# Four graph networks in one kernel: VectorE's next-tile work in front of the preceding tile's candidate

## The chip, the cores and the metric

The kernel runs on one core of one Trainium2 chip. The metric is the device time of one execution in microseconds; a lower time is better. Engines are called PE (TensorE, matmuls), DVE (VectorE), ACT (ScalarE), POOL (GpSimd) and SP (SyncE, which only issues transfers). Each has its own queue of instructions and works through it in order; they meet through semaphores.

## The reference

A graph has 12,500 nodes with 64 features and 212,500 edges (source, destination, type 0 to 3, weight). Four networks follow each other, each with a residual and a layer norm:

```python
x = layernorm(x + L0(x))   # 4 steps: a = segment_sum((x W_k + b_k)[type, src], dst); x = GRU(a, x)
x = layernorm(x + L1(x))   # 2 GIN convolutions: mlp(x + segment_sum(x[src], dst))
x = layernorm(x + L2(x))   # GCN: segment_sum(norm * (x W)[src], dst), relu, batch norm over all nodes
x = layernorm(x + L3(x))   # SAGE mean with edge weights

def _gru_cell(a, feat, w_ih, w_hh, b_ih, b_hh):
    gi = a @ w_ih.T + b_ih
    gh = feat @ w_hh.T + b_hh
    r, z = sigmoid(i_r + h_r), sigmoid(i_z + h_z)
    n = jnp.tanh(i_n + r * h_n)
    return (1.0 - z) * n + z * feat
```

All of it is a sum of source rows over the edges of each destination, and then a small dense part for each destination node.

## The kernel before

After a setup that sorts the edges into slots, the kernel makes nine passes (`p`), each over the 98 tiles (`NT`) of 128 destination nodes. Passes 0 to 3 are the four GRU steps, 4 to 6 the GIN layers, 7 is the GCN convolution, 8 the SAGE layer. Loops over tiles are unrolled.

One tile's sum has three sources. First, eight tiles ahead, PE picks source rows with one-hot matmuls into `ps_pair` (`oct_`, L1177, two for each step), ACT copies them to `raw_f` (`copy_pair`, L1479) and stores them to HBM in `bounce_f` (`move_out`, L1490). Six such steps make a group. SP loads a tile's 120 rows back in destination order into `thirds` (`load_msgs`, L791); ahead of a group's first tile it waits on SP's queue until all stores of the group have landed. Second, DVE splits these fp32 values into three bf16 parts: `split_rest` (L2050) makes the second part and waits for the load (`rows_back`), `split_low` (L2055) makes the third and reports `parts_made`. PE's `grid` (L1213) multiplies them with one-hots of the destination, which pass 0 makes on DVE (`make_grid`, L2013) and stores, which passes 1 to 3 load, and which later passes make anew. Third, edges that found no slot are gathered by POOL (L999) and summed by PE with left-over one-hots (`left_over_batch`, L1235), made on DVE by `make_left` (L2030, in pass 7 L2036 and L2040). The last of its four batches reports `tile_summed`.

Then comes the dense part, one tile behind. DVE adds the sums up (`take_sums`, L2081 in passes 0 to 3, L2094 in pass 7), PE turns them (`turn_sums`, L1252) and multiplies by the weights (`first_product`), ACT makes the gates with a tanh (L1530, `gate_done`), DVE makes the candidate's argument (`candidate`, L2162 and L2165), ACT its tanh (L1543, `cand_done`), and DVE mixes the new state (`finish`, L2177 and on). In pass 3 ACT loads a table ahead of the gate's tanh and another ahead of the square root of the layer norm. The new rows are split into three bf16 parts as well, by `late_parts`: its third entry, `low_of` (L2149), is in pass 3 the one that follows behind the candidate.

In pass 7 `candidate` is another computation: it waits for `gate_summed`, makes `o` (L2169), adds a bias row to `xs` (L2171), and ACT's relu of `o` (L1537) gives the row of `hs`. PE's `second_product` sums that row into the batch mean (L1294); in pass 7 it stands in PE's queue between the third and the fourth `left_over_batch`. In passes 4, 5, 6 and 8 `candidate` does nothing.

DVE's order is written out by hand in `one_tile`: with `at` as the tile whose sums PE makes, it takes the sums of `prev` (one back), does late parts of `older` (two back), and makes what PE needs for the next tile (`more`). In ACT's `one_tile` the order is: pair copy 0, turned copy, own rows, gate tanh or relu, candidate tanh, pair copy 1, store of the step.

Of the kernel before, what the change touches and what calls it, by code (L numbers as in the profile page):

```python
# [82 lines left out]
def build(nc, x, src, dst, edge_type, edge_weight, g_W, g_b, g_w_ih, g_w_hh, g_b_ih, g_b_hh,  # L83
# [53 lines left out]
    def tops(x):  # L137

        return x.rearrange("p x g f -> p (x g f)").bitcast(bf16).rearrange(
            "p (x g f o) -> p x g f o", x=3, f=H, o=2)[:, :, :, :, 1]  # L140
# [455 lines left out]
    def turns(at):  # L596
        return at.i * 6 + NT * len([q for q in range(at.p) if q != P_GIN2A]) + at.jj + 1
# [1081 lines left out]
    def _(dve):  # L1679
# [304 lines left out]
        def tile(t, at):  # L1984
            return t[:, ds(at.d(), 1), :].rearrange("p o f -> p (o f)")
# [13 lines left out]
        def make_grid(at, more):  # L1999
            if at.p in KEPT:  # L2000
                return
            if at.p == 0 and not (isinstance(at.i, int) and at.jj + more < 3):
                dve.wait_ge(doh_moved[at.slot3(more)], at.uses3(more) * 16)
                dve.sem_inc(dve_ran, 1)
            to = halves((doh_kept[at.slot3(more)] if at.p == 0 else doh_one[at.half(more)])[0:ROWS], GB)
            keep = dict(saturate=False) if at.p == 0 else {}
            lanes = dl_all[0:ROWS, ds(at.d(more), 1), :].rearrange("p o n -> p (o n)")
            if at.p == 0 and not isinstance(at.i, int):
                fixed = left_ws[0][0:ROWS].rearrange("p a g -> p (a g)")
                v.tensor_copy(fixed, lanes)  # L2010
                dve.drain()
                lanes = fixed
            last = v.tensor_tensor(to, numbers(ROWS, GB), spread(lanes, ROWS, GB), ALU.is_equal, **keep)  # L2013
            if at.p == P_SAGE:
                n, ws = (at.jj + more) % 3, edge_ws[at.half(more)][0:ROWS]
                dve.wait_ge(grec_landed[n], at.i * 32 + ((at.jj + more) // 3 + 1) * 16)
                for a in range(3):
                    v.tensor_copy(ws[:, a, :].rearrange("p (g o) -> p g o", o=2), twice(grec[n][0:ROWS, a, :], ROWS, GB))
                dve.drain()
                for a in range(3):  # L2020
                    last = v.tensor_tensor(halves(doh_three[at.half(more)][0:ROWS, a * GB * P:(a + 1) * GB * P], GB), to,  # L2021
                                           spread(ws[:, a, :], ROWS, GB), ALU.mult)
            last.then_inc(doh_made, 1)

        def make_left(at, more):
            rec, ws, hots = lrec[at.slot6(more)], left_ws[at.half(more)], loh_at[at.half(more)]
            dve.wait_ge(lrec_landed[at.slot6(more)], at.uses6(more + 6) * 16)
            if at.p < P_GIN1:
                for b in range(LB):
                    last = v.tensor_scalar(hots[:, b * K * P:(b + 1) * K * P], iota512[:, :],  # L2030
                                           rec[:, b, 2:3], None, ALU.is_equal)
                last.then_inc(loh_made, 1)
                return
            weights = range(3) if at.p == P_SAGE else ()
            for a, f in [(3, DL)] + [(a, W0 + a) for a in weights]:
                v.tensor_copy(ws[:, a, :].rearrange("p (g o) -> p g o", o=2), twice(rec[:, 0:LB, f], P, LB))  # L2036
            dve.drain()  # L2037
            plain = 3 if at.p == P_SAGE else 0
            to = [halves(hots[:, a * LB * P:(a + 1) * LB * P], LB) for a in range(4)]
            last = v.tensor_tensor(to[plain], numbers(P, LB), spread(ws[:, 3, :], P, LB), ALU.is_equal)  # L2040
            if at.p == P_SAGE:
                dve.drain()
                for a in weights:
                    last = v.tensor_tensor(to[a], to[3], spread(ws[:, a, :], P, LB), ALU.mult)
            last.then_inc(loh_made, 1)

        def split_rest(at, more):
            x = thirds[at.two(more)][0:ROWS]
            dve.wait_ge(rows_back[at.two(more)], at.backs(more) * 16)
            v.tensor_tensor(x[:, 1, :, :], x[:, 0, :, :], tops(x)[:, 0, :, :], ALU.subtract)  # L2050

        def split_low(at, more):
            x = thirds[at.two(more)][0:ROWS]
            dve.drain()
            v.tensor_tensor(x[:, 2, :, :], x[:, 1, :, :], tops(x)[:, 1, :, :], ALU.subtract).then_inc(parts_made, 1)  # L2055

        def take_state(at):
            if P_GIN1 <= at.p < P_SAGE:
                v.tensor_reduce(out=own_x[at.half()][:, :],
                                in_=tile(rows_now, at).rearrange("p (a f) -> p f a", a=3), axis=AX.X, op=ALU.add)  # L2060
            if at.p in (P_GIN2B, P_SAGE):
                v.tensor_copy(state[at.half()][:, 0:H], tile(hs if at.p == P_GIN2B else xs, at))
# [96 lines left out]
        def candidate(at):  # L2159
            if at.p < P_GIN1:  # L2160
                dve.wait_ge(gate_done, at.tiles(1))
                v.scalar_tensor_tensor(out=cand[:, :], in0=gate[:, 0:H], scalar=1.0, in1=ps_gate[:, 3 * H:4 * H],  # L2162
                                       op0=ALU.add, op1=ALU.mult)
                dve.drain()
                v.scalar_tensor_tensor(out=cand[:, :], in0=cand[:, :], scalar=0.5, in1=ps_gate[:, 2 * H:3 * H],  # L2165
                                       op0=ALU.mult, op1=ALU.add).then_inc(cand_made, 1)
            elif at.p == P_GCN:
                dve.wait_ge(gate_summed, turns(at))
                v.scalar_tensor_tensor(out=o[:, :], in0=ps_gate[:, 0:H], scalar=rsqrt_n[:, ds(at.d(), 1)],  # L2169
                                       in1=conv_b[:, :], op0=ALU.mult, op1=ALU.add).then_inc(o_biased, 1)  # L2170
                v.tensor_tensor(tile(xs, at), tile(xs, at), bn_beta[:, :], ALU.add)  # L2171
# [116 lines left out]
        def one_tile(at, careful=False):  # L2288
            p, known = at.p, isinstance(at.i, int)
            prev = None if known and at.jj == 0 else At(p, at.jj - 1, at.i)  # L2290
            older = None if known and at.jj < 2 else At(p, at.jj - 2, at.i)
            more = not (known and at.jj == NT - 1)
            if prev is not None:
                take_sums(prev, careful)
            if older is not None:
                late_parts[p][0](older)
            if more:
                make_grid(at, 1)
            if more and at.joined():
                split_rest(at, 1)  # L2300
            if older is not None:
                late_parts[p][1](older)
            take_state(at)
            if prev is not None:
                candidate(prev)
            if more:
                make_left(at, 1)
            if more and at.joined():
                split_low(at, 1)
            if older is not None:  # L2310
                late_parts[p][2](older)
            if prev is not None:
                finish(prev)
# [66 lines left out]
        for p in range(NPASS):  # L2380
# [18 lines left out]
            if p in range(1, P_SAGE):  # L2399
                for a in range(7):  # L2400
                    dve.wait_ge(rows_loaded[a], 16 * p)
            one_tile(At(p, 0))
            full = dve.value_load(any_full[0:1, 0:1], min_val=0, max_val=1)
            with dve.If(full < 1):
                long_loop(dve, p, 1, one_tile)
                take_sums(At(p, NT - 1))
            with dve.If(0 < full):
                by_six(dve, p, lambda at: one_tile(at, True), check_six)
                take_sums(At(p, NT - 1), True)
# [35 lines left out]
```

## Time and profile before

| | us |
|---|---|
| median of 3 runs | 9118.53 (9115.04 to 9126.54) |
| the profiled execution | 9112.42, span 9110.5 |
| busy, of the span | PE 72%, DVE 80%, ACT 41%, POOL 55% |
| chain that ended last | DVE 46%, DVEq 14%, PE 14%, DMA 11%, issue 8%, ACT 6% |

The span is the time from the first to the last instruction on record. Busy shares are means over passes with different limits; the chain that ended last says which engine the end was waiting for, followed back from the last instruction (DVEq is DVE's sequencer). What a change to one pass is worth is read from that pass's own rows.

### The profile page before, as it was taken

Reading aid. Unit: us, or ns where it says so; the run is one execution under the profiler, and the core shown is the slowest. Engines: PE = TensorE matmul, PEld = TensorE weight load, DVE = VectorE, ACT = ScalarE, POOL = GpSimd, SP = SyncE. Lnnn points to the kernel's source line nnn. Section 1 sums busy time; section 2 is a strip of 40 time slices with the busy share of each in tenths; the row PEclk is TensorE's granted clock in tenths of the full one; section 3 lists DMA queues with packets and bytes.
Section 4 is the critical chain, followed back from the end, with each engine's and each line's share of the span. In section 5 each row is a group of like instructions: output and inputs, shape, how many; then the busy total and the mean of one; then the engine's idle time right before and its main releaser. Section 6 shows DMA issues by size and latency. Waiting matters only on the chain.

```text
span 9110.5 us, 225080 instructions
## 1 busy us (share of the span) xinstructions
PE 6559.6 (72%) x82141; PEld 5404.3 (59%) x82142; DVE 7331.1 (80%) x16597; ACT 3714.5 (41%) x9508; POOL 5049.9 (55%) x4223
## 2 busy tenths in 40 slices
PE   3766676577777777777777778766667767748888
PEld 2333333477666666666666666655556656627777
DVE  8999999699977776776766678867779978859998
ACT  1444444444444444444666643321123322234443
POOL 2545455455545554554444457768877757744443
PEclk7999999899999999999888888978789989969999
DMA  3211121477778888888666778888788888848887
GB/s 90 74 60 53 54 64 53 141 195 195 196 214 221 219 225 223 220 220 227 177 175 177 182 217 236 241 229 218 217 228 209 212 220 231 235 123 221 216 219 182
DMA packets 1210397, 1665.55 MB, mean 183 GB/s; under 512 B 413276, under 2 KB 856575, under 8 KB 1206386
## 3 DMA queue, kind: packets, MB, share of 16 engines
q1 hardware_dynamic: 969618, 994.91, 41.9%
q10 hardware_dynamic: 126656, 482.46, 15.3%
q0 software_dynamic: 113056, 174.29, 9.8%
q8 instruction: 629, 10.31, 0.5%
q14 instruction: 438, 3.59, 0.1%
HBM read 1062.93 MB, written 588.17 MB: 181 GB/s over the span
## 4 chain that ended last, share of the span: by engine, by line
DVE 46%; DVEq 14%; PE 14%; DMA 11%; issue 8%; ACT 6%; POOL 2%; SPq 0%; ACTq 0%; POOLq 0%
DVE work L2055 8%; DMA work<-bounce_f 5%; DVE agg_sb L2081 4%; DVE work L2030 4%; DVE work L2013 4%; DVEq L2037 3%; DMA bounce_f<-work 3%; PE ps_agg L1213 3%; DVE hs L2021 2%; DVE work L2050 2%; PE ps_gate L1273 2%; DVE work L1822 2%; DVEq L1839 2%; ACT turned L1508 2%; PE ps_pair L1177 2%
## 5 line engine op out<-in xcount | busy, mean ns | idle before, releaser
L999 POOL DMA_INDIRECT work<-node_rows,work x3528 | 4203.4, 1191 | 3030.5 <-DMA work<-left_recs 1613.7
L1213 PE MATMUL ps_agg<-work 120*128 120x192 bf16 x12544 | 1348.5, 260 | 731.0 <-DVE work L2055 728.4
L1177 PE MATMUL ps_pair<-rows_now,work 128*128 128x64 bf16 x39168 | 1557.6, 201 | 141.2 <-DMA work<-src_onehots 69.7
L1213 PEld LDWEIGHTS ps_agg<-work 120*128 120x128 fp8e4 (+1 forms) x12544 | 1138.9, 101 | 809.8 <-issue 789.5
L1177 PEld LDWEIGHTS ps_pair<-rows_now,work 128*128 128x128 fp8e4 x39168 | 1477.4, 103 | 211.9 <-issue 160.3
L1479 ACT ACTIVATE work<-ps_pair 120x512 f32<-120x512 f32 x1632 | 954.2, 585 | 862.2 <-PE ps_pair L1177 750.0
L2050 DVE TENSOR_TENSOR work<-work 120x1024 f32<-120x1024 f32 x784 | 959.3, 1224 | 334.6 <-DMA work<-bounce_f 324.2
L2055 DVE TENSOR_TENSOR work<-work 120x1024 f32<-120x1024 f32 x784 | 961.8, 1227 | 75.8 <-issue 4.5
L1235 PE MATMUL ps_agg<-work 128*128 128x192 bf16 (+1 forms) x7840 | 901.9, 260 | 166.1 <-DMA work<-node_rows,work 165.9
L2013 DVE TENSOR_TENSOR work<-iota_bf,dl_all 120x2048 bf16<-120x2048 bf16 (+1 forms) x588 | 824.2, 1402 | 27.9 <-SPq L746 15.3
L1235 PEld LDWEIGHTS ps_agg<-work 128*128 128x128 bf16 x7840 | 672.5, 104 | 198.7 <-issue 157.2
L2081 DVE TENSOR_TENSOR agg_sb<-agg_sb,ps_agg 128x256 f32<-128x256 f32 x1176 | 493.5, 420 | 65.0 <-PE ps_agg L1235 3.7
L953 POOL TENSOR_SCALAR work<-work 128x36 f32<-128x36 f32 x49 | 90.6, 1850 | 784.8 <-PE ps_pair L1105 567.0
L2162 DVE SCALAR_TENSOR_TENSOR cand<-gate,ps_gate 128x64 f32<-128x64 f32 x392 | 86.4, 220 | 514.8 <-ACT gate L1530 511.8
L2030 DVE TENSOR_SCALAR work<-iota,work 128x512 bf16<-128x512 int16 x1568 | 493.0, 377 | 0.8 <-issue 0.7
L1483 ACT ACTIVATE work<-ps_pair 120x384 bf16<-120x384 f32 x816 | 368.4, 485 | 272.9 <-PE ps_pair L1190 260.7
L1508 ACT ACTIVATE turned<-ps_turn 128x384 f32<-128x384 f32 (+2 forms) x784 | 316.2, 403 | 373.0 <-PE ps_turn L1264 241.0
L1273 PE MATMUL ps_gate<-state_w,turned 69*128 69x256 f32 x784 | 304.1, 473 | 226.3 <-ACT turned L1508 226.3
L1221 PE MATMUL ps_agg<-work,hs 120*128 120x192 bf16 x4704 | 454.5, 246 | 5.3 <-DMA work<-bounce 2.9
L1447 ACT ACTIVATE work<-hs,ones_f 128x480 fp8e4<-128x480 bf16 x392 | 409.4, 1137 | 8.1 <-ACT hs L1439 4.2
L1221 PEld LDWEIGHTS ps_agg<-work,hs 120*128 120x128 bf16 x4704 | 393.3, 97 | 8.8 <-issue 3.2
L955 POOL TENSOR_SCALAR work<-hs 128x36 f32<-128x36 f32 x196 | 387.3, 2033 | 0.0
(345 smaller groups left out, 11715.8 us busy)
## 6 DMA issues: line engine op xcount, KB each, us to landing
bounce_f<-work ACTq DMA_DIRECT2D x816, 480.0 KB
work<-bounce_f SPq DMA_DIRECT2D x784, 480.0 KB
work<-src_onehots SPq DMA_DIRECT2D x918, 256.0 KB
bounce<-work ACTq DMA_DIRECT2D x102, 727.5 KB
work<-bounce SPq DMA_DIRECT2D x98, 727.5 KB
work<-dst_onehots SPq DMA_DIRECT2D x294, 240.0 KB
work<-node_rows,work POOLq DMA_INDIRECT x3528
hs<-grid_vals SPq DMA_DIRECT2D x49, 960.0 KB, 5.0
```

Source lines behind the costliest of these rows:

```text
L999: pool.indirect_dma_start(out=ring[:, at.slot6() * LB + b, 0:3 * H], out_offset=None, in_=table_of(at.p), in_offset=bass.IndirectOffsetOnA ...
L1177: last = mm(to[:, a * H:(a + 1) * H], oh[s.buf()][:, EIGHT * m + a, :], rows_now[:, s.chunk() * CHUNK + EIGHT * m + a, x * H:(x + 1) * H], ...
L1213: last = mm(acc[:, to:to + 3 * H], hot, tops(thirds[at.two()])[0:ROWS, :, b, :], start=b == 0 or p < P_GIN1 and b == GB // 2, stop=False)
L1221: mm(acc[:, 0:3 * H], doh_three[at.half()][0:ROWS, (a * GB + b) * P:(a * GB + b + 1) * P], msgs[at.jj % 3][0:ROWS, k, s, 0:3 * H], start=a ...
L1235: last = mm(acc[:, k * AGG:k * AGG + n], hot, ring[:, u * LB + b, 0:n], start=False, stop=end and (p >= P_GIN1 or k % 2 == 1))
L1479: a_(raw_f[s.raw()][0:ROWS, 2 * m:2 * m + 2, :, :], ps_oct[s.bank(m)][0:ROWS, :].rearrange("p (i b f) -> p i b f", i=2, b=SB), ACT.Copy).t ...
L1508: a_(to, frm, ACT.Copy).then_inc(turned_copied, 1)
L2013: last = v.tensor_tensor(to, numbers(ROWS, GB), spread(lanes, ROWS, GB), ALU.is_equal, **keep)
L2030: last = v.tensor_scalar(hots[:, b * K * P:(b + 1) * K * P], iota512[:, :], rec[:, b, 2:3], None, ALU.is_equal)
L2050: v.tensor_tensor(x[:, 1, :, :], x[:, 0, :, :], tops(x)[:, 0, :, :], ALU.subtract)
L2055: v.tensor_tensor(x[:, 2, :, :], x[:, 1, :, :], tops(x)[:, 1, :, :], ALU.subtract).then_inc(parts_made, 1)
L2081: last = v.tensor_tensor(to, to, typed[:, :, x * H:(x + 1) * H], ALU.add)
```

## The change

In DVE's `one_tile`, the block that makes the next tile's left-over one-hots (`make_left`) and its second split (`split_low`) is now ahead of the candidate of the preceding tile; before, it was behind it.

```diff
@@ -2301,12 +2301,12 @@
             if older is not None:
                 late_parts[p][1](older)
             take_state(at)
-            if prev is not None:
-                candidate(prev)
             if more:
                 make_left(at, 1)
             if more and at.joined():
                 split_low(at, 1)
+            if prev is not None:
+                candidate(prev)
             if older is not None:
                 late_parts[p][2](older)
             if prev is not None:
```

No instruction is added, removed or resized, and no semaphore changes its count. The other engines' queues are as they were.

## Rows read from the trace of the kernel before

**Rows 1.** Waits of DVE, whole span: line, releaser, us, times, longest.
```profile
DVE cand L2162 <- ACT gate L1530: 511.8, 310, 3.5
```

**Rows 2.** Windows, passes 0, 1, 3, 7: length, busy (xtiles), PEclk, DMA share, GB/s.
```profile
1760.00:2600.00 840.00, 20.62 (x93) 0.92 0.72 197
2720.00:3400.00 680.00, 18.60 (x84) 1.00 0.80 220
...
4340.00:5200.00 860.00, 19.07 (x86) 0.85 0.69 176
...
7450.00:8000.00 550.00, 31.14 (x87) 0.92 0.87 233
```

**Rows 3.** Timeline of DVE, pass 1: start, us, line; idle before in brackets.
```profile
2906.10 1.45 DVE L2081 TENSOR_TENSOR agg_sb<-agg_sb,ps_agg 128x256 f32<-128x256 f32 x3
...
2907.60 1.22 DVE L2050 TENSOR_TENSOR work<-work 120x1024 f32<-120x1024 f32 x1
...
2910.43 0.22 DVE L2162 SCALAR_TENSOR_TENSOR cand<-gate,ps_gate 128x64 f32<-128x64 f32 x1 [1.47 <-ACT gate L1530]
2910.73 0.22 DVE L2165 SCALAR_TENSOR_TENSOR cand<-cand,ps_gate 128x64 f32<-128x64 f32 x1
2910.87 1.39 DVE L2030 TENSOR_SCALAR work<-iota,work 128x512 bf16<-128x512 int16 x4
2912.35 1.23 DVE L2055 TENSOR_TENSOR work<-work 120x1024 f32<-120x1024 f32 x1
2913.49 0.22 DVE L2177 TENSOR_TENSOR delta<-state,cand_t 128x64 f32<-128x64 f32 x1
...
2914.23 0.91 DVE L2081 TENSOR_TENSOR agg_sb<-agg_sb,ps_agg 128x256 f32<-128x256 f32 x2
```

**Rows 4.** Waits of DVE in pass 0 alone, 1744 to 2640 us.
```profile
DVE cand L2162 <- ACT gate L1530: 17.3, 21, 2.2
```

**Rows 5.** Timeline of the other engines, pass 1, the same tile and its neighbour.
```profile
2907.61 0.33 PE L1252 MATMUL ps_turn<-eye,agg_sb 128*128 128x128 f32 x1 [0.48 <-DVE agg_sb L2081]
...
2910.98 0.26 ACT L1543 ACTIVATE cand_t<-cand 128x64 f32<-128x64 f32 x1 [0.58 <-DVE cand L2165]
...
2911.83 0.32 ACTq L1490 DMA_DIRECT2D bounce_f<-work  x1
...
2913.72 1.52 PE L1213 MATMUL ps_agg<-work 120*128 120x192 bf16 x16 [0.91 <-DVE work L2055]
```

**Rows 6.** Timeline of ACT and of DVE at a group's start, pass 7.
```profile
7672.87 0.32 ACTq L1490 DMA_DIRECT2D bounce_f<-work  x1
...
7684.15 1.23 DVE L2050 TENSOR_TENSOR work<-work 120x1024 f32<-120x1024 f32 x1 [2.63 <-DMA work<-bounce_f]
```

**Rows 7.** One window in and behind that wait, pass 7; columns PE, PEld, DVE, ACT, POOL.
```profile
7683.00:7690.00 7.00, 4.04 (x42) 3.66 (x40) 5.52 (x11) 1.34 (x3) 3.59 (x4) 0.61 1.02 285
```

**Rows 8.** Timeline of DVE, one tile of pass 3.
```profile
4799.25 1.41 DVE L2081 TENSOR_TENSOR agg_sb<-agg_sb,ps_agg 128x256 f32<-128x256 f32 x3
...
4804.62 0.22 DVE L2162 SCALAR_TENSOR_TENSOR cand<-gate,ps_gate 128x64 f32<-128x64 f32 x1 [2.03 <-ACT gate L1530]
...
4809.15 1.41 DVE L2081 TENSOR_TENSOR agg_sb<-agg_sb,ps_agg 128x256 f32<-128x256 f32 x3
```

**Rows 9.** Timeline of DVE, PE and ACT, one tile of pass 7.
```profile
7603.11 0.28 DVE L2169 SCALAR_TENSOR_TENSOR o<-ps_gate,rsqrt_n,conv_b 128x64 f32<-128x64 f32 x1
...
7603.43 0.42 DVE L2036 CAST work<-work 128x8 bf16<-128x8 f32 x1
...
7604.00 0.25 PE L1235 MATMUL ps_agg<-work 128*128 128x192 bf16 x1
...
7604.26 0.36 ACTq L1490 DMA_DIRECT2D bounce_f<-work  x1
...
7604.45 1.22 DVE L2055 TENSOR_TENSOR work<-work 120x1024 f32<-120x1024 f32 x1
...
7605.76 0.36 DVE L2094 TENSOR_REDUCE agg_sb<-ps_agg 128x64 f32<-128x192 f32 x1
```

## The prediction

> **What bounds the kernel now.** I read four views in this order. The waits of VectorE (DVE) come first: its one large wait inside the passes is for ScalarE's gate tanh, just in front of the candidate, 511.8 us over 310 tiles [rows 1]. Four windows of steady stretches give each pass its period as length by count: 840/93 = 9.03 us a tile in pass 0, 680/84 = 8.10 in pass 1 (pass 2 is its twin), 860/86 = 10.00 in pass 3, 550/87 = 6.32 in pass 7 [rows 2]. The other passes have no candidate, so the edit leaves their order alone. The timeline of one tile of pass 1 then shows a closed loop: DVE takes the sums at 2906.10, is out of work 1.47 us before the gate at 2910.43, and starts the next sums at 2914.23 without waiting for them, 8.13 us later [rows 3]. So in passes 1 to 3 the way sums, turn (PE), copy (ACT), product (PE), gate (ACT), back to DVE sets the period, with DVE's remaining work behind it. In pass 0 DVE has its one-hot grid to make in between, and waits for the gate only 17.3 us in all [rows 4].
>
> **Part 1: one-hots and second split move ahead of the candidate, passes 1 and 2.** Nothing is added or removed; on DVE only the order of two blocks changes, and no DMA is issued by either. Times from the start of the sums, t0. The moved block starts where DVE falls idle, at 2910.43 - 1.47 = 2908.96, t0 + 2.8 or so. From L2030 to the step behind L2055 it takes 2913.49 - 2910.87 = 2.62 us, more than the 1.47 us wait, so the candidate starts at about t0 + 5.4 and never waits for its gate (which was there at t0 + 4.33) [rows 3]. Gain: 1.47. The new cost: `finish` now stands directly behind the candidate and needs ScalarE's tanh of it. L2165 to the tanh is 0.25 us, the tanh 0.26 [rows 3, 5], and some 0.03 back: 0.54 us from L2165 to L2177, where L2165 to L2030 took 0.14. Cost 0.40. An instruction that doesn't wait also starts 0.08 before its predecessor ends (L2030 at 2910.87, L2165 until 2910.95), which the waiting one loses. By DVE alone the tile takes 8.13 - 1.47 - 0.08 + 0.40 = 6.98 us. PE fits: of its 8.13 us it waits 0.91 for the split and 0.48 for the sums [rows 5], so it has 6.7 us of work at full clock, 0.25 under the new period.
>
> What is late next is not on DVE. ScalarE's queue holds, behind the candidate's tanh, the second pair copy and the store of a step's rows to `bounce_f` (L1490), 0.85 us after the tanh starts [rows 5]. Every sixth tile the SP queue may load the next group only when that store has landed, and DVE's first split two tiles on needs the load. Today the store goes out at 2911.83, 2.40 us before the next sums, and the split comes 8.13 + 1.50 us after those: 12.0 us are available [rows 3, 5]. After the change the tanh starts at t0 + 5.95, the store at 6.80, only 0.17 before the next sums: 0.17 + 6.98 + 1.50 = 8.65 us are available. What the round trip takes shows in pass 7 under like traffic: store at 7672.87, the split that waited for its data at 7684.15, 11.3 us [rows 6]. So 2.7 us are lost every sixth tile, 0.44 a tile: 7.42. Such a stall leaves PE idle, and in pass 7 the granted clock after a wait of this kind is 0.61 of full speed over 7 us, mostly the 1.2 GHz level [rows 7]; pass 1, with PE's short waits of today, is at the 2.4 GHz level throughout (1.00 [rows 2]). With 0.25 us of slack PE then holds DVE up by 1 to 2 us: I add 0.2 a tile. Estimate 7.62 us against 8.10, gain 0.48 x 97 tiles x 2 passes = 93 us. Bounds: 6.98 (no stall, 109 a pass) and 8.1 (nothing).
>
> The Trainium skill would have it otherwise. In "DMA: Bandwidth & Descriptors", section "Anatomy of one DMA", a transfer costs about 2.0 us and its bytes at 436 GB/s; for the 120 x 1024 fp32 of a step an estimate by that page is 3.1 us each way, 6.3 for both, and no stall at all. The trace disagrees: 11.3 us [rows 6], with the DMA engines at 0.87 of the time [rows 2]. The measured one is used; the page's result is rival B.
>
> **Part 2: pass 3.** The wait for the gate is 2.03 us in a tile of 4809.15 - 4799.25 = 9.90 [rows 8], because its gate also sits behind a table load. The moved block, 2.5 us as before, takes its place, and here `low_of` stands between candidate and `finish` and hides part of the tanh: cost 0.26 instead of 0.40, by one slot of 0.14. 9.90 - 2.03 - 0.08 + 0.26 = 8.05, if the gate, there at t0 + 5.37, comes before the moved block ends at t0 + 5.6. The mean period of 10.00 holds tiles with a slow PE clock (0.85 [rows 2]); with the gate off the path most of that goes. DMA need rises from 0.69 to 0.69 x 10.00/8.15 = 0.85, just bearable. I take 8.15: 1.85 x 97 = 180 us gained. Bounds: 190 (8.05 throughout) and 130 (a period of 8.65, PE's slow tiles staying).
>
> **Part 3: pass 0** pays the 0.40 and has little wait to give back: 0.40 x 98 = 39, less 17.3 [rows 4] = 21 us lost (bounds 5 and 40).
>
> **Part 4: pass 7.** Here the candidate is `o`, its consumer ScalarE's relu, and behind that PE's mean product, which PE issues ahead of the last left-over product that ends the tile's sum. Now: `o` at 7603.11, last product 7604.00 to 7604.25, next sums 7605.76; DVE is never waiting and the sum is 1.5 us early [rows 9]. After: L2055 starts 0.32 earlier (what L2169 and L2171 took), at 7604.13, `o` 1.14 later at 7605.27, which is 2.16 later than now; the tile's sum ends 2.16 later too, 7606.41, next sums 7606.47 instead of 7605.76. That is 0.71 us a tile, a wait of DVE for PE that did not exist. The store moves with the relu from 1.50 us ahead of the sums to 0.05 ahead while the period grows 0.71, so the group's stall grows by 0.74, 0.12 a tile. 0.83 x 98 = 81; DMA is less loaded at the longer period, so I take 75 us lost (bounds 40 and 95).
>
> **Sum.** +21 - 93 - 180 + 75 = -177 us. The profiled execution took 9112.4 us with a span of 9110.5; the median of the runs is 9118.5. The change scales neither the 2 us around the span nor the setup, so it is taken off the median: 9118.5 - 177 = 8941, say 8940.
>
> **Rivals.** A, the above, 50%. B, the group's round trip shrinks or hides and passes 1 and 2 reach 6.98: 21 - 218 - 180 + 55 = -322, 8800 us, 15%. For it: today's regular loads are never waited for in pass 1. Against it: the 11.3 us [rows 6]. C, DMA and PE's clock eat the gain of passes 1 and 2 altogether and pass 3 gives 140: 21 + 0 - 140 + 80 = -39, 9080 us, 22%. For it: 0.80 x 8.10/6.98 = 0.93 of DMA time would be needed, and no steady stretch shows over 0.87 [rows 2]. D, slower: PE's clock. PE needs 6.7 us a tile at 2.4 GHz [rows 5] and at most twice that, 13.4, at 1.2 GHz. If stalls hold it low for 30% of passes 1 to 3 the tile takes 8.7: 2 x 0.6 x 97 = +116, pass 3 -126, passes 0 and 7 +96 as above, sum +86, 9205 us. It decides from about a quarter of the time on; the clocks of 0.85 and 0.92 in passes 3 and 7 mean 30 and 16% [rows 2], pass 1 shows none. 8%. The Trainium skill speaks for D: "TensorE: Matmul & The Clock Gate", "HAM oscillation", warns that a loop that waits for a transfer each round starts each round cold. The trace agrees for one round [rows 7], but here it is one tile in six. E, the order changes and the wait only changes its name (the tanh copy waits as long as the gate did): 9118, 5%; against it ScalarE is idle ahead of that tanh [rows 5].
>
> A and B are faster, C mostly (0.2% is 18 us, about what a measurement of this kernel can tell from no change): faster 0.86, same 0.06, slower 0.08. Range 8820 to 9085: A with its bounds, C, and the part of B where a stall of a microsecond is left; B's far end and D stay out, under 2 in 10.
>
> **What would show it.** DVE's wait in front of L2162 gone in passes 0 to 3 and one of about 0.3 us at L2177 from ScalarE's tanh (part 1). L2050 waiting for `bounce_f` every sixth tile of passes 1 and 2, 2 to 4 us (if absent, B). Periods 9.2, 7.6, 8.15 and 7.1 us. In pass 7 a wait of DVE's L2094 for PE's L1235. Granted clock under 1.00 in passes 1 and 2, nearer 1.00 in pass 3. It would be wrong if the round trip is far from 11 us, or if in pass 3 ScalarE's table loads come back onto the path.

## The result: 8867 us, and the profile after

| | before | after |
|---|---|---|
| median of 4 runs each, us | 9117.24 (9115.04 to 9126.54) | 8866.99 (8864.22 to 8878.84) |
| the profiled execution, us | 9112.42, span 9110.5 | 8868.43, span 8866.5 |

The ratio is 0.9726, with a 95% interval from 0.9709 to 0.9743: 250 us faster, where 177 were forecast. The spans differ by 244 us. To see where they went, each pass is measured from the start of its first sums (L2081, in passes 4 to 8 L2094) to the start of its last, 97 tiles later. The same table holds the experiments below (us, one profiled execution each):

| kernel | pass 0 | 1 | 2 | 3 | 4 | 5 | 6 | 7 |
|---|---|---|---|---|---|---|---|---|
| before | 879.2 | 781.8 | 781.7 | 973.2 | 651.1 | 645.4 | 703.9 | 613.2 |
| after | 901.6 | 717.8 | 708.8 | 796.8 | 645.8 | 647.3 | 701.9 | 662.2 |
| e1_gcn_old | 901.4 | 721.7 | 722.4 | 794.9 | 637.3 | 644.1 | 704.5 | 606.7 |
| e2_store_first | 901.1 | 700.6 | 700.0 | 796.1 | 648.9 | 638.8 | 702.6 | 670.8 |
| e3_half | 870.0 | 691.1 | 698.8 | 871.3 | 664.5 | 639.2 | 705.6 | 617.3 |
| e4_light_dma | 902.6 | 681.8 | 688.7 | 797.0 | 644.3 | 643.7 | 702.2 | 658.1 |
| e5_tanh_twice | 914.1 | 700.8 | 702.2 | 811.9 | 650.0 | 644.4 | 704.7 | 650.5 |
| e6_before_light | 882.3 | 773.0 | 770.6 | 973.6 | 638.2 | 638.0 | 705.2 | 603.0 |
| f1_split_behind | 869.7 | 689.4 | 683.0 | 793.7 | 658.6 | 652.3 | 701.9 | 612.7 |
| f2_store_too | 866.4 | 689.6 | 693.1 | 795.5 | 657.0 | 641.9 | 705.4 | 606.6 |
| g1_before_store | 884.2 | 783.7 | 780.0 | 975.0 | 663.9 | 647.5 | 708.9 | 617.0 |
| g2_before_swap | 882.9 | 786.6 | 784.7 | 973.4 | 651.4 | 648.4 | 710.5 | 619.4 |

Passes 4 to 6, which no kernel here changes, show the scatter of such a number: up to 27 us in pass 4, 14 in pass 5, 9 in pass 6. Passes 1 and 2 scatter as well: e1 has the order of after in them (717.8 and 721.7, 708.8 and 722.4 us), f1 that of e3 (691.1 and 689.4, 698.8 and 683.0). So a difference of 15 us in one pass shows nothing by itself. The kernels also ran at different times and on different chips: the before that ran beside them took 9117 us beside after, 9125 beside e1 to e4, 9110 beside e5, e6, f1 and f2, and 9139 beside g1 and g2. Ratios are taken against that one, and are the better comparison between experiments. Between before and after, pass 0 lost 22 us, passes 1 and 2 won 64 and 73, pass 3 won 176, pass 7 lost 49. That is 242 of the 244.

The waits of VectorE (line, releaser, us in all, times, longest) answer [rows 1]:

```profile
DVE work L2050 <- DMA work<-bounce_f: 407.2, 230, 31.5
DVE agg_sb L2094 <- PE ps_agg L1235: 113.2, 114, 4.2
DVE delta L2177 <- ACT cand_t L1543: 112.4, 389, 0.3
...
DVE cand L2162 <- ACT gate L1530: 23.7, 11, 3.7
```

The wait for the gate fell from 511.8 us to 23.7. Three others grew: for ScalarE's tanh, at 0.29 us each in all four GRU passes; for PE's sums, where the prediction put it (28.2 us in before); and for the loads from `bounce_f`, which before took 324.2 us over 134 waits.

The windows of steady stretches answer [rows 2] (length; busy and count of L2165, in pass 7 of L2094; PE clock; DMA share; GB/s). First passes 0, 1, 2 and 3, then pass 7:

```profile
1800.00:2600.00 800.00, 18.84 (x85) 0.88 0.73 190
2720.00:3400.00 680.00, 20.39 (x92) 0.97 0.91 243
3480.00:4140.00 660.00, 19.95 (x90) 0.97 0.93 247
4220.00:4980.00 760.00, 20.57 (x93) 0.92 0.83 220
```
```profile
7150.00:7750.00 600.00, 31.44 (x88) 0.84 0.84 216
```

Periods are 717.8/97 = 7.40 us in pass 1, 708.8/97 = 7.31 in pass 2, 796.8/97 = 8.21 in pass 3, 662.2/97 = 6.83 in pass 7 and 901.6/97 = 9.29 in pass 0. The DMA engines now work at 0.91 to 0.93 of the time in passes 1 and 2, above all that before had shown [rows 2].

One undisturbed tile of pass 2 stands against [rows 3] (timeline of DVE: start, us, line, idle before and releaser):

```profile
3580.30 1.40 DVE L2081 TENSOR_TENSOR agg_sb<-agg_sb,ps_agg 128x256 f32<-128x256 f32 x3
...
3581.75 1.22 DVE L2050 TENSOR_TENSOR work<-work 120x1024 f32<-120x1024 f32 x1
...
3583.02 1.14 DVE L2030 TENSOR_SCALAR work<-iota,work 128x512 bf16<-128x512 int16 x4
3584.25 1.23 DVE L2055 TENSOR_TENSOR work<-work 120x1024 f32<-120x1024 f32 x1
3585.39 0.21 DVE L2162 SCALAR_TENSOR_TENSOR cand<-gate,ps_gate 128x64 f32<-128x64 f32 x1
3585.68 0.22 DVE L2165 SCALAR_TENSOR_TENSOR cand<-cand,ps_gate 128x64 f32<-128x64 f32 x1
3586.22 0.22 DVE L2177 TENSOR_TENSOR delta<-state,cand_t 128x64 f32<-128x64 f32 x1 [0.32 <-ACT cand_t L1543]
...
3586.97 1.41 DVE L2081 TENSOR_TENSOR agg_sb<-agg_sb,ps_agg 128x256 f32<-128x256 f32 x3
```

The block fills the place of the wait, L2162 runs at once, and L2177 starts 0.54 us after L2165: as forecast. The tile takes 6.67 us, not the 6.98 of the sum. Most of that is seen in the row of L2030: its four instructions take 1.14 us here from the first's start to the last's end, 1.39 in [rows 3].

A group's start in pass 2 (ScalarE's store, SP's load, and the split that waits for it) answers [rows 6]:

```profile
3480.20 0.32 ACTq L1490 DMA_DIRECT2D bounce_f<-work  x1
```
```profile
3485.55 0.34 SPq L791 DMA_DIRECT2D work<-bounce_f  x1
```
```profile
3490.78 1.23 DVE L2050 TENSOR_TENSOR work<-work 120x1024 f32<-120x1024 f32 x1 [2.17 <-DMA work<-bounce_f]
```

This round trip takes 10.58 us. "Round trip" is here the time from the issue of a group's last store to the start of the first split that uses its rows; it holds two transfers, the wait on SP's queue and DVE's wait. Over 15 groups of a pass (without the first and the last) its mean is 10.2 in pass 1 and 10.1 in pass 2, and the idle time in front of the split is 1.45 and 1.36 us, where before had 0.00. In pass 7 the round trip went from 11.4 us before to 9.6 after, and the idle time from 2.39 to 1.15.

A tile of pass 3 of after (DVE) answers [rows 8], and one of pass 7 (several engines) [rows 9]:

```profile
4502.29 1.41 DVE L2081 TENSOR_TENSOR agg_sb<-agg_sb,ps_agg 128x256 f32<-128x256 f32 x3
4503.62 0.15 DVE L2122 RECIPROCAL rstd<-std 128x1 f32<-128x1 f32 x1
...
4507.94 0.21 DVE L2162 SCALAR_TENSOR_TENSOR cand<-gate,ps_gate 128x64 f32<-128x64 f32 x1
4508.23 0.22 DVE L2165 SCALAR_TENSOR_TENSOR cand<-cand,ps_gate 128x64 f32<-128x64 f32 x1
4508.37 0.22 DVE L2149 TENSOR_TENSOR stage<-left_over,stage 128x64 bf16<-128x64 f32 x1
4508.77 0.23 DVE L2177 TENSOR_TENSOR delta<-state,cand_t 128x64 f32<-128x64 f32 x1 [0.19 <-ACT cand_t L1543]
```
```profile
7302.56 1.23 DVE L2055 TENSOR_TENSOR work<-work 120x1024 f32<-120x1024 f32 x1
7303.70 0.28 DVE L2169 SCALAR_TENSOR_TENSOR o<-ps_gate,rsqrt_n,conv_b 128x64 f32<-128x64 f32 x1
...
7304.01 0.26 ACT L1537 ACTIVATE hs<-o 128x64 f32<-128x64 f32 x1 [3.39 <-DVE o L2169]
...
7304.32 0.43 PE L1294 MATMUL ps_agg<-hs,mean_f 128*128 128x64 f32 x2 [2.16 <-ACT hs L1537]
...
7304.59 0.25 PE L1235 MATMUL ps_agg<-work 128*128 128x192 bf16 x1
...
7304.86 0.32 ACTq L1490 DMA_DIRECT2D bounce_f<-work  x1
7304.88 0.36 DVE L2094 TENSOR_REDUCE agg_sb<-ps_agg 128x64 f32<-128x192 f32 x1 [0.77 <-PE ps_agg L1235]
```

In pass 3 the candidate no longer waits, and what is left of the tanh is 0.19 us, since L2149 lies in between. In pass 7 the chain is the one that was forecast, link by link: `o` behind L2055, relu, mean product, last left-over product, sums, each waiting for the one above; the store goes out at the sums and not 1.50 us ahead of them.

### The profile page after: what moved, and what is told of

It reads as the page before. It is cut to its first block, busy times and chain, and to the rows that moved or that the text cites. A ratio compares the mean times of both kernels' runs of the same rounds, so it can differ in the third digit from the quotient of the medians.

```text
span 8866.5 us, 225080 instructions
## 1 busy us (share of the span) xinstructions
PE 6555.1 (74%) x82141; PEld 5433.4 (61%) x82142; DVE 7299.7 (82%) x16597; ACT 3712.4 (42%) x9508; POOL 5050.2 (57%) x4223
## 4 chain that ended last, share of the span: by engine, by line
DVE 45%; DMA 16%; DVEq 14%; PE 11%; issue 8%; ACT 3%; POOL 2%; SPq 1%; ACTq 0%; POOLq 0%
DMA work<-bounce_f 9%; DVE work L2055 7%; DMA bounce_f<-work 4%; DVE work L2013 4%; DVE work L2050 4%; DVE work L2030 3%; DVE agg_sb L2081 3%; DVEq L2037 3%; PE ps_agg L1213 3%; DVE hs L2021 3%; PE ps_pair L1177 2%; POOL work L999 2%; DVE work L1822 2%; DVEq L1839 2%; DVE work L1814 2%
## 5 line engine op out<-in xcount | busy, mean ns | idle before, releaser
L999 POOL DMA_INDIRECT work<-node_rows,work x3528 | 4211.5, 1194 | 2765.1 <-DMA work<-left_recs 1310.3
L1177 PE MATMUL ps_pair<-rows_now,work 128*128 128x64 bf16 x39168 | 1582.9, 202 | 143.4 <-DMA work<-src_onehots 71.0
L1213 PE MATMUL ps_agg<-work 120*128 120x192 bf16 x12544 | 1369.6, 262 | 371.4 <-DVE work L2055 370.7
L1177 PEld LDWEIGHTS ps_pair<-rows_now,work 128*128 128x128 fp8e4 x39168 | 1502.5, 104 | 218.1 <-issue 166.8
L2050 DVE TENSOR_TENSOR work<-work 120x1024 f32<-120x1024 f32 x784 | 957.5, 1221 | 418.1 <-DMA work<-bounce_f 407.2
L2055 DVE TENSOR_TENSOR work<-work 120x1024 f32<-120x1024 f32 x784 | 961.6, 1226 | 75.9 <-issue 4.5
L2081 DVE TENSOR_TENSOR agg_sb<-agg_sb,ps_agg 128x256 f32<-128x256 f32 x1176 | 493.1, 419 | 79.7 <-PE ps_agg L1235 13.2
L1273 PE MATMUL ps_gate<-state_w,turned 69*128 69x256 f32 x784 | 299.2, 466 | 230.5 <-ACT turned L1508 230.5
L2030 DVE TENSOR_SCALAR work<-iota,work 128x512 bf16<-128x512 int16 x1568 | 460.3, 356 | 0.1
L1543 ACT ACTIVATE cand_t<-cand 128x64 f32<-128x64 f32 x392 | 100.5, 256 | 737.5 <-DVE cand L2165 733.4
```

Of the source, the lines that this page charges most:

```text
L999: pool.indirect_dma_start(out=ring[:, at.slot6() * LB + b, 0:3 * H], out_offset=None, in_=table_of(at.p), in_offset=bass.IndirectOffsetOnA ...
L1177: last = mm(to[:, a * H:(a + 1) * H], oh[s.buf()][:, EIGHT * m + a, :], rows_now[:, s.chunk() * CHUNK + EIGHT * m + a, x * H:(x + 1) * H], ...
L1213: last = mm(acc[:, to:to + 3 * H], hot, tops(thirds[at.two()])[0:ROWS, :, b, :], start=b == 0 or p < P_GIN1 and b == GB // 2, stop=False)
L2081: last = v.tensor_tensor(to, to, typed[:, :, x * H:(x + 1) * H], ALU.add)
```

## Experiments

**e1_gcn_old: pass 7 alone as before.** Does the loss of pass 7 hang on its own order, and is it independent of the other passes?

```diff
+            if prev is not None and p in (7,):
+                candidate(prev)
             if more:
                 make_left(at, 1)
             if more and at.joined():
                 split_low(at, 1)
-            if prev is not None:
+            if prev is not None and p != 7:
                 candidate(prev)
```

> Kernel after, but pass 7 keeps the order of before. Theory: the late relu behind the moved block holds PE's mean product and the tile's last left-over product, which alone cost pass 7 49 us (its first to last sums are 662.2 us apart now, 613.2 before). Then 8867 - 49 = 8818 us, period of pass 7 back at 6.32 us, no wait of L2094 for L1235 there beyond that of before. Rival, pass 7 is slower because it starts in another state (loads and store order left by the passes ahead): 8867, period 6.8.

8814.53 us median (8799.12 to 8826.37), ratio 0.9651 (0.9634 to 0.9668). Pass 7 takes 606.7 us, 55 less than after, and its clock and DMA share are back:

```profile
7150.00:7700.00 550.00, 31.49 (x88) 0.93 0.88 236
```

The loss is this pass's own, and the change without pass 7 is better than the whole.

**e2_store_first: the store ahead of the tanh.** If the group's wait comes from the store's place in ScalarE's queue, an earlier store should remove it.

```diff
@@ one_tile of ScalarE, ahead of the candidate's tanh (passes 1, 2) or of the relu (7); shortened:
@@ the same two calls behind the tanh are skipped in these passes
+            if at.p in (1, 2) and s is not None:
+                one_pair(1)
+                move_out(s)
```

> Kernel after, but in passes 1 and 2 ScalarE makes the second pair copy and the step's store behind the gate's tanh and in front of the candidate's, and in pass 7 in front of the relu. Theory of the late store: DVE's split waits for bounce_f at 15 of 15 group starts of passes 1 and 2 (1.4 us each) because the store follows a tanh that now comes late; with the store 1.4 us earlier the waits fall under 0.4 us, periods of passes 1 and 2 go from 7.40 and 7.31 to about 7.1, that of pass 7 from 6.83 to 6.6: 8867 - 29 - 20 - 22 = 8796 us. Rival, the DMA engines are simply full (0.9 and over in those passes) and the wait only moves to other tiles: within 10 us of 8867.

8866.4 us median (8839.09 to 8895.71), ratio 0.9724 (0.9701 to 0.9747): no gain that the medians show, where 70 us were expected. The store now goes out 1.4 us ahead of the next sums instead of 0.2. Yet the idle time in front of a group's split fell only from 1.45 and 1.36 us to 1.04 and 1.09 in passes 1 and 2, and the time from a group's last store to its first load rose from 5.2 and 5.1 us to 5.6 and 5.7: a store that starts earlier is landed only partly earlier. And the copy and the issue now hold the tanh up, so DVE's wait for it grew from 0.32 to 0.47 us a tile in these passes, some 14 us a pass:

```profile
DVE delta L2184 <- ACT cand_t L1543: 139.5, 389, 1.8
```

(L2177 is L2184 here; 112.4 us in after.) All in all passes 1 and 2 won 17 and 9 us in the profiled execution, which was the fastest of the four. In pass 7 the idle time did shrink, from 1.15 to 0.40 us, but the median period rose from 6.57 to 6.92: the relu now stands behind the copy, and `o`'s chain to the sums is the limit there. In both places a wait was traded for another.

**e3_half: one-hots ahead of the candidate, split behind it.** This hides the tanh behind L2055 and keeps pass 7's `o` from waiting for the split.

```diff
             if more:
                 make_left(at, 1)
+            if prev is not None:
+                candidate(prev)
             if more and at.joined():
                 split_low(at, 1)
-            if prev is not None:
-                candidate(prev)
```

> Kernel after, but only the one-hots stand ahead of the candidate; the second split stands behind it again, between candidate and finish, in all five passes. Theory: the split covers ScalarE's tanh, so the 0.32 us wait at L2177 goes, and in pass 7 the relu comes 1.3 us earlier, ahead of the point at which PE holds DVE up. Pass 0 about 8.85 us a tile (from 9.30, -44), passes 1 and 2 -25 each, pass 7 back at 6.35 (-47), pass 3 slower, since its gate comes at t0 + 5.4 and the one-hots end at 4.5: 8.7 instead of 8.21 (+48). Sum 8867 - 93 = 8774 us. Rival, the tanh's 0.3 us are hidden by DMA waits anyway: passes 0 to 2 unchanged, 8867 - 47 + 48 = 8868.

8842.05 us median (8828.79 to 8855.58), ratio 0.9688 (0.9669 to 0.9707): 25 us less than after, where 93 were expected. Pass 0 won 32 of the 44 and pass 7 45 of the 47; pass 3 lost 75 instead of 48, and passes 1 and 2 won 27 and 10 instead of 25 each. The wait for the gate is partly back, in passes 1 to 3 (0.3, 0.4 and 1.0 us a tile):

```profile
DVE work L2050 <- DMA work<-bounce_f: 415.7, 217, 30.2
DVE cand L2162 <- ACT gate L1530: 178.0, 223, 4.0
```

So each pass has its own best place. Where the gate comes late (pass 3, [rows 8]) both blocks must stand in front. Where it is never waited for (pass 0) the split should stay behind and hide the tanh. In passes 1 and 2 the two waits cancel, 0.32 us of tanh for 0.31 and 0.36 of gate, and what was won there was won elsewhere (f1).

**e4_light_dma: an eighth of the kept one-hots.** Passes 1 to 3 load only an eighth of `dst_onehots`, so the sums use part of old one-hots; all instructions and waits stay. Is the rest of the wait one for DMA bandwidth?

```diff
-            sp.dma_start(doh_kept[at.slot3(more)][0:ROWS], dst_onehots.ap()[ds(at.d(more) * ROWS, ROWS), :]
+            sp.dma_start(doh_kept[at.slot3(more)][0:ROWS, 0:GB * P // 8],
+                         dst_onehots.ap()[ds(at.d(more) * ROWS, ROWS), 0:GB * P // 8]
```

> Kernel after, but passes 1 to 3 load only an eighth of each tile's kept destination one-hots (30 KB for 240; the rest of the computation runs on what lay there). It leaves out 12% of those passes' DMA bytes and nothing of the engines' work. Theory, the round trip of store and load stretches with the DMA load: it falls from 10.2 us to under 9, the waits at group starts in passes 1 and 2 vanish, periods 7.05: 8867 - 34 - 25 = about 8805 us, pass 3 unchanged. Rival, a fixed latency: waits of 1.4 us stay, 8867. Second rival, DVE would be at 6.7 if DMA let it: 6.75 in both, 8750.

8813.63 us median (8806.58 to 8818.73), ratio 0.9657 (0.9641 to 0.9674). Passes 1 and 2 won 36 and 20 us, pass 3 nothing; nearly all of it came out of L2050's waits for loads (0.33 and 0.22 us a tile). The round trip fell from 10.2 and 10.1 to 9.2 and 9.5 us, and the idle time to 0.66 and 1.02, so the waits did not vanish, as was expected. So its length hangs on what else is moved: 210 KB less a tile, of 243 GB/s x 7.40 us = 1.8 MB, shortened it by 0.6 to 1.0 us.

**e5_tanh_twice: the exposed tanh made longer.** A second tanh of the same shape ahead of the real one, into a buffer that is free then.

```diff
+                a_(hidT[:, 0:H], cand[:, :], ACT.Tanh)
                 a_(cand_t[:, :], cand[:, :], ACT.Tanh).then_inc(cand_done, 1)
```

> Kernel after, with the candidate's tanh computed twice on ScalarE (the first result goes nowhere). Theory: the tanh stands alone between candidate and finish, so a second one of 0.16 to 0.26 us is paid in full by passes 0 and 3 and mostly by 1 and 2: +0.2 x 98 x 4 = +80, about 8945 us; the wait at L2177 grows from 0.32 by that much. Rival, the exposure is hidden by what comes later: under +20.

8887.27 us median (8869.50 to 8890.87), ratio 0.9754 (0.9727 to 0.9780): 20 us over after by the medians, 26 by the ratios, where 78 were expected. The wait grew, but by 0.15 us a tile, not by the duration of 0.26:

```profile
DVE delta L2178 <- ACT cand_t L1544: 169.7, 390, 0.5
```

(L2178 and L1544 are L2177 and L1543 of after, with 112.4 us over 389 waits.) An instruction of ScalarE that waits for nothing starts before its predecessor ends: in after, the pair copy starts 0.16 us behind a tanh of 0.26 us (3585.94 and 3586.10). That is the price of a second one. Pass 0 lost 12.5 us and pass 3 15.1, which is 0.13 and 0.16 a tile: there the tanh is on the path. Passes 1 and 2 lost nothing (-17 and -7, which is within the scatter): a longer tile left 0.65 and 0.88 us of idle time in front of the group's split instead of 1.45 and 1.36. There a nanosecond on DVE is paid back by a wait for the load. The profiled execution was the fastest of the four, 18 us under their median, so the losses of its passes are rather too small.

**e6_before_light: the light load in the kernel before.** The control for e4: the edit of e4 in before.

> Kernel before, with passes 1 to 3 loading only an eighth of each tile's kept destination one-hots (the rest computes on what lay there). Theory: before the change the loop through gate and candidate bound these passes and no transfer was waited for, so 12% less DMA traffic gives nothing: within 10 us of the kernel before, period 8.07. Rival, DMA load lengthened that loop already (the gathers, the lists of left-overs): 40 us or more faster.

9091.02 us median (9071.97 to 9104.79), ratio 0.9979 (0.9967 to 0.9991), 19 us faster than before on the same chip, where under 10 were expected; the table has 9 and 11 us in passes 1 and 2. What little it gave fits L2030, whose four instructions took 1.21 and 1.20 us from start to end on the mean instead of 1.33 and 1.32, while no wait of DVE shrank by more than 0.01 us a tile. Before, the splits of the 15 groups did not wait for their loads in these passes; the 56 us of e4 came out of just these waits, so they are the new order's.

**f1_split_behind: each pass its own place.** Passes 0 to 2 have only the one-hots ahead of the candidate, pass 3 both, pass 7 neither.

```diff
+            if prev is not None and p == 7:
+                candidate(prev)
             if more:
                 make_left(at, 1)
+            if prev is not None and p in (0, 1, 2):
+                candidate(prev)
             if more and at.joined():
                 split_low(at, 1)
-            if prev is not None:
+            if prev is not None and p in (3, 4, 5, 6, 8):
                 candidate(prev)
```

> The order that each pass liked best so far: passes 0 to 2 with the one-hots ahead of the candidate and the second split behind it, pass 3 as in the kernel after, pass 7 as in the kernel before. Theory: the gains are separate, each bound by its own pass. From the after kernel: pass 0 -32, passes 1 and 2 -27 and -10, pass 3 0, pass 7 -50: about 8750 us. Rival, the DMA engines (0.9 and over in passes 1 and 2) give later passes back what they gained: 8790 or more.

8736.87 us median (8722.53 to 8747.43) beside 9109.73 of before on the same chip, ratio 0.9582 (0.9555 to 0.9609): faster than both kernels. A tile of pass 2 (DVE):

```profile
3480.19 1.14 DVE L2030 TENSOR_SCALAR work<-iota,work 128x512 bf16<-128x512 int16 x4
3481.75 0.22 DVE L2162 SCALAR_TENSOR_TENSOR cand<-gate,ps_gate 128x64 f32<-128x64 f32 x1 [0.42 <-ACT gate L1530]
3482.04 0.22 DVE L2165 SCALAR_TENSOR_TENSOR cand<-cand,ps_gate 128x64 f32<-128x64 f32 x1
3482.36 1.22 DVE L2055 TENSOR_TENSOR work<-work 120x1024 f32<-120x1024 f32 x1
3483.50 0.22 DVE L2177 TENSOR_TENSOR delta<-state,cand_t 128x64 f32<-128x64 f32 x1
```

The tanh is hidden and 0.42 us of the gate's wait are back, so the undisturbed tile is no shorter: 6.77 us, 6.67 in after. Still passes 1 and 2 win 28 and 26 us on after. The tanh, and the store behind it, go out earlier in the tile (the store 1.1 us ahead of the next sums instead of 0.2), and DVE's idle time fell by 0.15 and 0.13 us a tile in front of L2050 and by 0.07 in front of the sums, where it waits for PE. That the early store is the cause is not shown: e3 has the same order in these passes and won 27 and 10 us, but kept 1.41 and 1.75 us of idle time in front of a group's split, where f1 has 0.91 and 1.08.

**f2_store_too: f1 with the early store of e2 in passes 1 and 2.**

> The kernel before this one in the list, and in passes 1 and 2 ScalarE's second pair copy and the step's store also ahead of the candidate's tanh. Theory of the late store: it goes out some 0.4 us earlier than the tanh would let it, and the group waits of 1.4 to 1.75 us shrink by as much: passes 1 and 2 -7 each, 8735 us. Rival: the copy and the issue (0.9 us on ScalarE) now delay the tanh past the split, which costs 0.2 us a tile: +40, 8790 us.

8726.66 us median (8714.19 to 8743.68), ratio 0.9575 (0.9545 to 0.9605), not to be told from f1. The two passes it edits took 689.6 and 693.1 us beside 689.4 and 683.0, and the idle time in front of a group's split did not shrink (1.16 and 1.32 us). With e2 that makes twice that an earlier store, paid for with a later tanh, brought little or nothing.

**g1_before_store and g2_before_swap: why L2030 got shorter.** In before's passes 1 and 2 the last of the four L2030 often takes 0.55 us instead of 0.35. Each time POOL's issue of an indirect transfer (L999) ends inside it, and in 145 of the 197 long ones ScalarE's store starts there too. g1 is before with the early store, g2 before with L2055 in front of L2030; both in passes 1 and 2 alone. The edit of g2:

```diff
+            if more and at.joined() and p in (1, 2):
+                split_low(at, 1)
             if more:
                 make_left(at, 1)
-            if more and at.joined():
+            if more and at.joined() and p not in (1, 2):
                 split_low(at, 1)
```

> The kernel before, with the second pair copy and the store of a step in front of the candidate's tanh in passes 1 and 2. In the trace of before, the last of the four L2030 takes 0.50 instead of 0.35 us there, whenever POOL's L999 ends 0.35 to 0.45 us after it starts; the store L1490 falls inside the same instruction, so the trace alone can't say which of the two stretches it. Theory P (POOL's L999 does it): the store is moved, POOL is not, the four L2030 stay at about 1.39 us, passes 1 and 2 stay at 8.0 to 8.1 us a tile and the time within 15 us of before. Theory S (the store does it): the four L2030 fall to 1.14 us, 0.25 us a tile, 194 tiles, some 45 us faster than before.

> The kernel before, with the second split L2055 in front of the left-over one-hots L2030 in passes 1 and 2, both still behind the candidate. L2030 then starts 1.2 us later against the rest of the tile. Theory P or S (something that happens at that moment stretches L2030): the four L2030 fall from 1.39 to 1.14 us, the period from 8.06 to 7.8 us, 0.25 x 194 = 48 us faster than before (9065 beside 9115). Rival (L2030 is slow in itself when it stands behind the candidate, or the period is set elsewhere, by PE or the gate): L2030 or the period stay, within 15 us of before. If L2055 is stretched instead of L2030, by as much, the time stays as well; its 1.23 us in the timeline tells.

g1: 9136.54 us median (9108.44 to 9153.41) beside 9139.15 of before, ratio 0.9996 (0.9980 to 1.0011). The period did not change, and its four L2030 (L2037 in its own numbering) take 1.33 and 1.32 us on the mean, as in before. In the tile shown they take 1.38 us, though the store now starts 0.66 us behind it and not 0.96 as in before (2918.95 and 2919.91), which is ahead of the last of the four; L999 ends at 2952.80 + 0.94 = 2953.74, L2037 at 2952.48 + 1.38 = 2953.86:

```profile
2952.48 1.38 DVE L2037 TENSOR_SCALAR work<-iota,work 128x512 bf16<-128x512 int16 x4
2952.80 0.94 POOL L999 DMA_INDIRECT work<-node_rows,work  x1 [0.30 <-issue]
2953.14 0.32 ACTq L1490 DMA_DIRECT2D bounce_f<-work  x1
...
2960.55 1.14 DVE L2037 TENSOR_SCALAR work<-iota,work 128x512 bf16<-128x512 int16 x4
```

g2: 9147.60 us median (9116.41 to 9169.65), ratio 1.0009 (0.9996 to 1.0023), where 48 us less were expected. L2030 did become shorter, 1.21 and 1.22 us for four on the mean instead of 1.33 and 1.32, but the period did not (8.11 and 8.09 us beside 8.06): the rival, that the period is set elsewhere, held. The split no longer makes PE wait, and PE's wait for the sums is one long one instead of two short ones (0.91 and 0.48 [rows 5]):

```profile
2919.84 0.33 PE L1252 MATMUL ps_turn<-eye,agg_sb 128*128 128x128 f32 x1 [1.40 <-DVE agg_sb L2081]
...
2921.51 0.77 PE L1274 MATMUL ps_gate<-typed_v,turned 128*128 128x192 f32 x2
2922.07 0.85 PE L1275 MATMUL ps_gate<-typed_v,turned 128*128 128x192 f32 x2
```
```profile
2923.26 0.22 DVE L2162 SCALAR_TENSOR_TENSOR cand<-gate,ps_gate 128x64 f32<-128x64 f32 x1 [2.07 <-ACT gate L1530]
```
```profile
2720.00:3400.00 680.00, 18.39 (x83) 0.92 0.82 218
```

Behind it PE runs slower (0.77 and 0.85 us for what takes 0.49 in tiles without such a wait), the gate comes late (2.07 us of wait instead of 1.47 [rows 3]), and the granted clock of pass 1 is 0.92 where before had 1.00 [rows 2], so between the 1.2 and the 2.4 GHz level. In both passes 62 of the 97 tiles ran at full clock throughout, and took 7.96 and 7.97 us on the mean, 0.1 less than before's 8.06; the 35 with a clock under 0.9 took 8.38 and 8.30. So DVE's gain went into the tiles in which PE ran slow. All ten executions of g2 show it, with a mean clock of 0.886 to 0.894 over the whole kernel, where the 19 of before beside them had 0.896 to 0.908.

## Why the forecast was right in direction and 73 us short

**Part 1, passes 1 and 2: 93 us forecast, 137 measured (64 + 73).** The forecast of 7.62 us a tile was 6.98 for DVE, 0.44 for loads, 0.20 for PE. The mechanism was right: the gate's wait went, the tanh's came at the 0.54 us from L2165 to L2177, and a new wait for `bounce_f` stands at every group's start. The term that failed is the 6.98. The undisturbed tile takes 6.67, 0.31 less: 0.25 in L2030, 0.05 between L2081 and L2050 (1.45 us instead of the 1.50 of [rows 3]).

The forecast took L2030's 1.39 us for its duration, but it is stretched there, as in most tiles of before's passes 1 and 2 (the median is 1.39, too). On the mean the four take 1.33 and 1.32 us from start to end in before and 1.15 in after, 0.17 x 194 tiles = 34 of the 44 us that were missed. g1 shows that the store is not the cause, and before does too: none of the 190 L2030 in which a store starts, but no L999 ends, is stretched. That it is POOL rests on the match in the traces, since no run here moved POOL: of the 1568 L2030 of before, 197 took over 0.43 us, and all of these ended 0.105 to 0.125 us behind the end of an L999. So did the 202 of g1 and the 106 of after. The new order puts L2030 where an L999 seldom ends late inside it in passes 1 and 2, by luck. In pass 0 the stretch remains (1.24 us before and after).

The store-to-load term came out near its size by two errors. At a group's start the idle time is 1.45 and 1.36 us, not 2.7, because the round trip took 10.2 and 10.1 us and not the 11.3 of pass 7: it was taken to be fixed and is not (e4, and pass 7 itself, at 9.6 us after). But other tiles wait too. All waits of L2050 for `bounce_f` within the pass are 52.5 us in pass 1 and 45.2 in pass 2, which is 0.54 and 0.47 us a tile, 0.07 and 0.06 of it there before; 0.44 was forecast.

The 0.20 for PE's clock was too large. DVE's idle time in front of the sums, where such a delay shows, grew from 0.16 to 0.23 us a tile, by 0.07. The clock is at 0.97 in these windows: 82 and 84 of the 97 tiles run at full clock and take 7.28 and 7.20 us on the mean, so all that the slower ones add to 7.40 and 7.31 is 0.12 and 0.11, and part of that is the load that they waited for. The term's excess of 0.13 is 25 us over both passes; with the 34 of L2030 that is more than the 44 missed, and small waits that the forecast left out take the difference.

**Part 2, pass 3: 180 us forecast, 176 measured.** 8.05 us for the undisturbed tile, 8.06 in the median; the mean of 8.21 stands beside 8.15. L2177 starts 0.40 us behind L2149 (4508.37 to 4508.77) and not 0.14: the tanh costs 0.26, as summed. The clock came only half of the way towards 1.00, from 0.85 to 0.92.

**Part 3, pass 0: 21 us lost in the forecast, 22 measured.** e3 and f1 show the same from the other side: with the split behind the candidate, the pass takes 870 us, 32 less than after and 9 less than before.

**Part 4, pass 7: 75 us lost in the forecast, 49 measured.** The chain through relu, mean product and last left-over product is there at its size: the median period went from 5.87 to 6.57 us, 0.70 where 0.71 was forecast, and e1 takes it back. The step that failed is "the group's stall grows by 0.74": it shrank from 2.39 to 1.15 us. The store is indeed later against the sums (0.02 us ahead of them at 7304.86, forecast 0.05), but the round trip shrank by 1.8 us. Fewer bytes were asked for in a microsecond (216 GB/s instead of 233 [rows 2]), and e4 shows that less traffic shortens it; that this is the reason here is not shown by a run of its own. Over all tiles L2050's idle time fell by 0.11 us a tile where +0.12 was forecast: 0.23 x 97 = 22 of the 26 us. The forecast also had DVE never waiting in this pass; in fact `o` waited for PE 8.2 us in all before, and after it does not.

**The rivals.** B wanted passes 1 and 2 at 6.98 us and the round trip hidden. The tile can be shorter than that, but the round trip is not hidden, so B's mechanism is false. The Trainium skill, "DMA: Bandwidth & Descriptors", section "Anatomy of one DMA", stood behind it with an estimate of 6.3 us for store and load; the measured 9.2 to 11.4 us do not bear that out. The section's figures are for transfers that GpSimd issues, though, and these two are issued by ScalarE and SyncE, which the prediction did not say. C saw a ceiling at a DMA share of 0.87; the engines hold 0.91 to 0.93 over 660 us and more. D, the slower one, did not happen: the clock of passes 1 and 2 is 0.97. Its price of 8.7 us was also reckoned too high: it doubles the time of 30% of the tiles, while the 30% read from a clock of 0.85 are a share of the time, and by time 6.7 us of work become 6.7/0.85 = 7.9, less than the 8.10 of before. Nor are the 6.7 us all work, since PE waits 0.58 us a tile in them for ScalarE's copy in front of L1273. The effect is real all the same, as g2 shows at 0.92, where it ate the whole of a small gain. E is refuted: the gate's wait of 511.8 us became 23.7, and the tanh's, which was to take its place, is 112.4.

## What to carry to other kernels

When a block is moved into a wait, ask stage by stage whether it is longer than the wait: what it is longer by pushes back everything behind it, such as another engine's chain (pass 7) or a store that a later load needs (passes 1 and 2), and the best place can differ in each stage (f1: 373 us less than before, where the whole move gives 250). Take the duration of an instruction from its undisturbed rows, not from one tile: it may be stretched in most of them. A round trip through HBM gets shorter and longer with the traffic around it, so a stall that it causes can give back a delay (e5, passes 1 and 2) and eat part of a gain (e2).

## What the runs showed of the hardware

- DVE and POOL: when L999, which issues an indirect transfer, ends 0.30 to 0.50 us after the start of an L2030 (128 x 512, int16 to bf16), that L2030 takes 0.43 to 0.59 us instead of 0.35 and ends 0.116 us (median) behind L999. L2050 and L2055, fp32 with two inputs, keep their 1.22 us on the mean. The Trainium skill, "SBUF — State Buffer", section "Terms", has the two share a pair of ports that one holds for a whole instruction while the other waits; the trace agrees in that the wait ends with the other engine's end, but L999 mostly runs 0.94 us and disturbs only near its end: 584 of the 781 L2030 of before that overlap an L999 stay under 0.40 us.
- A higher DMA load than before was sustained: 243 to 247 GB/s at a share of 0.91 to 0.93 over 660 us and more.
- An earlier store lands only partly earlier: in e2, with the store 1.2 us earlier against the sums, the time from store to load grew by 0.4 to 0.6 us.
- With one PE wait for DVE of mostly 1.39 us a tile the granted clock was 0.92, with two of 0.91 and 0.44 us it was 1.00 (medians, g2 beside before), though PE's idle time was smaller in all: 1.55 us a tile instead of 1.92. The Trainium skill, "TensorE: Matmul & The Clock Gate", section "HAM oscillation — how this bites in real kernels", tells of loops whose rounds each wait and start cold; 35 of the 97 tiles of each pass of g2 agree, though their wait is for DVE and not for a transfer.
